# Slots made of two units of 256 edges in a graph kernel's gather stages, with attention's running totals added on TensorE

## The reference

```python
x = x + _L0_gnn_ref(_layernorm(x), src, dst, edge_weight, ...)   # segment_sum(val * n[dst], src), then a 256x256 matmul
x = x + _L0_ffn_ref(_layernorm(x)[None], ...)[0]                 # 16 experts, best 2
x = x + _L1_gnn_ref(_layernorm(x), ..., edge_attr_3, edge_index) # attention over edges, below
x = x + _L1_ffn_ref(_layernorm(x)[None], ...)[0]                 # 8 experts, best 1

# _L1_gnn_ref, H = 8 heads of D = 32
h_src = h[src]; h_dst = h[dst]
alpha = (h_src * a_src).sum(-1) + (h_dst * a_dst).sum(-1)
alpha = alpha + (relu(edge_attr @ edge_W.T + edge_b) * h_dst).sum(-1)
alpha = where(alpha >= 0, alpha, 0.2 * alpha)
ex = exp(alpha - segment_max(alpha, dst)[dst])
attn = ex / maximum(segment_sum(ex, dst)[dst], 1e-10)
out = segment_sum(h_src * attn, dst) + bias
```

## Time and profile before

| | us |
|---|---|
| median of 3 runs | 3073.1 |
| lowest, highest | 3066.4, 3090.2 |
| profiled execution | 3098.1 |
| its span | 3096.4 |
| PE busy (share of the span) | 2038.6 (66%) |
| DVE busy | 1689.1 (55%) |
| POOL busy | 1249.9 (40%) |
| ACT busy | 819.5 (26%) |
| `message_rows` | about 134 to 906 |
| `message_sums` | about 926 to 1151 |
| `attention` | about 1701 to 2625 |

### The profile page before, as it was taken

The page is one execution under the profiler, slowest core; times in us unless marked ns, Lnnn a source line. Parts: engine busy times, 40 slices in busy tenths (PEclk is TensorE's granted clock), DMA queues, the critical chain, the costliest instruction groups (busy, mean ns, idle before and its releaser), DMA issues. The chain is left out here.

```text
span 3096.4 us, 41327 instructions
## 1 busy us (share of the span) xinstructions
PE 2038.6 (66%) x12463; PEld 1551.3 (50%) x12552; DVE 1689.1 (55%) x3274; ACT 819.5 (26%) x2162; POOL 1249.9 (40%) x1222
## 2 busy tenths in 40 slices
PE   0256566555539996699623276667777766896995
PEld 0144444443427775599512155555555555235995
DVE  7644444444437778655576177666766767503222
ACT  5222222222210002233214033222333332432331
POOL 1166666666650000355303556456656651001221
PEclk9977676777769998799856588888988988898998
DMA  2144444444348862422321344344444442400113
GB/s 67 64 145 152 154 161 152 153 150 144 134 139 281 295 226 74 143 71 72 101 65 58 114 122 122 111 117 131 121 117 119 125 115 60 151 9 19 37 37 103
DMA packets 192121, 366.13 MB, mean 118 GB/s; under 512 B 47573, under 2 KB 102632, under 8 KB 191525
## 3 DMA queue, kind: packets, MB, share of 16 engines
q1 hardware_dynamic: 135472, 207.05, 20.9%
q0 software_dynamic: 56160, 156.43, 16.5%
q10 hardware_dynamic: 274, 0.00, 0.0%
HBM read 232.23 MB, written 131.07 MB: 117 GB/s over the span
## 5 line engine op out<-in xcount | busy, mean ns | idle before, releaser
L1945 POOL DMA_INDIRECT att_rows<-hdram,top_ix x488 | 502.2, 1029 | 375.6 <-DVE att_msg L2173 229.6
L767 POOL DMA_INDIRECT mtab<-msgs_rw,msgs_ix x488 | 486.6, 997 | 377.3 <-ACT msgs_rw L729 207.9
L656 PE MATMUL msgs_p_m<-nodes_n,msgs_hott 128*128 x976 | 364.1, 534 | 57.9 <-issue 42.5
L2017 PE MATMUL att_p_acc<-att_msg,att_hot 128*128 128x264 f32 x976 | 306.8, 468 | 100.6 <-ACT att_msg L2055 45.7
L589 DVE TENSOR_TENSOR msgs_rw<-msgs_p_m,msgs_sorted 128x1024 f32<-128x1024 f32 x122 | 149.3, 1224 | 376.2 <-remote 183.4
L656 PEld LDWEIGHTS msgs_p_m<-nodes_n,msgs_hott 128*128 128x128 f32 x976 | 248.9, 268 | 127.3 <-issue 82.1
L2017 PEld LDWEIGHTS att_p_acc<-att_msg,att_hot 128*128 128x128 f32 x976 | 211.1, 227 | 156.4 <-issue 88.6
L2047 ACT ACTIVATE att_enc<-att_p_z 128x1024 f32<-128x1024 f32 x122 | 124.8, 1023 | 586.8 <-remote 315.5
L2124 DVE TENSOR_TENSOR att_enc<-att_enc,att_p_h 128x1024 f32<-128x1024 f32 x122 | 148.8, 1219 | 224.2 <-remote 171.2
L837 PE MATMUL sums_part<-sums_rows,sums_hot 128*128 128x256 f32 x976 | 224.6, 390 | 34.0 <-DVE sums_hot L812 33.8
L1359 PE MATMUL exp_y<-exp_own,exp_ht 128*128 128x256 f32 x1032 | 239.0, 379 | 2.4 <-issue 2.4
(11 more groups left out here) (375 smaller groups left out, 3558.8 us busy)
## 6 DMA issues: line engine op xcount, KB each, us to landing
sums_rows<-mtab SPq DMA_DIRECT2D x122, 520.0 KB, 4.6
etab<-msgs_et SPq DMA_DIRECT2D x122, 288.0 KB
att_hz<-etab SPq DMA_DIRECT2D x122, 288.0 KB
first_w<-in_L_ffn_w SPq DMA_DIRECT2D x16, 512.0 KB
ffn0x_w<-in_L_ffn_w SPq DMA_DIRECT2D x16, 512.0 KB
ffn_w<-in_L_ffn_Wd SPq DMA_DIRECT2D x8, 1024.0 KB, 10.6
mtab<-msgs_rw,msgs_ix POOLq DMA_INDIRECT x488
att_rows<-hdram,top_ix POOLq DMA_INDIRECT x488
```

Source lines behind the costliest of these rows:

```text
L656: last = T.matmul(p_m[g % 2][:, q, :], hott[g % 2][:, q, :], node, start=True, stop=True)
L767: nc.gpsimd.indirect_dma_start(mtab, bass.IndirectOffsetOnAxis(ap=ix[:, g, q:q + 1], axis=0), rw[g % RS][:, q, :], None).then_inc(s_free[g ...
L1945: nc.gpsimd.indirect_dma_start(rows[:, g % RS, q, :], None, hdram, bass.IndirectOffsetOnAxis(ap=ix1[:, g, q:q + 1], axis=0)).then_inc(s_ro ...
L2017: last = T.matmul(p_acc[g % 2][:, 0:HW], hot[g % 2][:, q, :], msg[g % 2][:, q, :], start=(q == 0), stop=(q == G - 1))
```

## The change

A slot still has 512 edges and 4 columns, but it is two units of 256 edges (`U` = 2, `UE` = 256), and the two may belong to two different tiles. Tiles are padded to a multiple of 256 and not of 512, so that 220 units in `NS` = 110 slots do for the `dst` side. The `src` side keeps its 122 slots. What follows:

- `window_columns` and `window_rows` make the columns of the plan twice for `dst`, once for each unit of a slot. `gb` and the starts have one row of 110 for each unit.
- `message_rows`: SP loads a slot's records with two DMAs of half the size. PE reads two tile numbers for each slot, and the first two columns' matmuls take the one tile, the last two the other.
- `attention`, scores: likewise two tile numbers, `destinations` and `offsets` take two tiles. `maxima` compares 8 units and the one before (8 x 8 x 9 = 576 elements), and first makes the matrix of which units have different tiles (two small operations), which was made for all batches at the stage's start.
- `attention`, sums: `gathered` is gone from DVE. Each unit has its own PSUM buffer. PE adds the two columns of a unit and then the tile's old total, out of `acc`, by one more float32 matmul with the identity (`past`). For a batch's first unit the old total is the one that DVE multiplied by the fall (`fade`, once for a batch). ACT's `keep_total` copies each unit's PSUM buffer into `acc`, two copies for a slot, and at a batch's last unit one more into `total`.
- The order on ACT and PE is another: ACT does `weights` first, `keep_total` of the earlier slot's units before and behind `encodings`; PE does `past` of a slot's second unit between `encoders` and `destinations`, and `sums` ahead of `edge_tops`. `sums` waits until both units' copies of the slot before are done.

```diff
+U = 2
+UE = GE // U
+NS = ((E + NT * (UE - 1)) // UE + U - 1) // U
...
# window_columns
-    link(V.tensor_scalar(cmp[:], ends[:], ip, None, ALU.is_le))
+    for h in range(parts):
+        link(V.tensor_scalar(turn[:], cst["ip"][:], float(parts), float(h), ALU.mult, ALU.add))
+        link(V.tensor_scalar(cmp[:], ends[:], turn[:, 0:1], None, ALU.is_le))
...
# message_rows, load
-                sp.dma_start(sorted1[:, g, :], tab1[bass.ds(at, GE), :].rearrange("(p q) r -> p (q r)",
-                                                                                 p=P)).then_inc(s_tile[g % 8], 16)
+                for h in range(U):
+                    at = sp.value_load(starti[0:1, h * NS + g:h * NS + g + 1], min_val=0, max_val=E)
+                    sp.dma_start(sorted1[:, g, h * G // U * 8:(h + 1) * G // U * 8],
+                                 tab1[bass.ds(at, UE), :].rearrange("(p q) r -> p (q r)", p=P)).then_inc(s_tile[g % 8], 16)
...
# message_rows, products
+                for h in range(U):
+                    b = pe.value_load(gb[0:1, h * NS + g:h * NS + g + 1], min_val=0, max_val=NT - 1)
+                    nodes.append(n[:, bass.ds(b, 1), :].rearrange("p a c -> p (a c)"))
...
# attention, tensor
-                if g >= 2:
-                    pe.wait_ge(s_add, g - 1)
+                if g:
+                    pe.wait_ge(s_kept, U * g)
                 for q in range(G):
-                    last = T.matmul(p_acc[g % 2][:, 0:HW], hot[g % 2][:, q, :], msg[g % 2][:, q, :],
-                                    start=(q == 0), stop=(q == G - 1))
-                last.then_inc(s_acc, 1)
+                    T.matmul(p_acc[q * U // G][:, 0:HW], hot[g % 2][:, q, :], msg[g % 2][:, q, :],
+                             start=(q * U % G == 0), stop=False)
+                past(U * g)
+
+            def past(u):
+                if u % BU == 0:
+                    pe.wait_ge(s_faded, u // BU + 1)
+                    old = faded[:]
+                else:
+                    pe.wait_ge(s_kept, u)
+                    old = acc[:, bass.ds(held.pop(u), 1), :].rearrange("p a c -> p (a c)")
+                T.matmul(p_acc[u % U][:, 0:HW], cst["ident"][:], old, start=False, stop=True).then_inc(s_acc, 1)
...
# attention, tensor, the order of a step
+                if 0 <= s - LAG - 1 < NS:
+                    past(U * (s - LAG - 1) + 1)
+                if s + 1 < NS:
+                    nodes = destinations(s + 1)
...
# attention, scalar
-            def keep_total(g):
+            def keep_total(u):
...
-                act.wait_ge(s_add, g + 1)
-                if g:
-                    act.wait_ge(s_kept, g)
-                S.copy(acc[:, bass.ds(b, 1), :].rearrange("p a c -> p (a c)"), total[g % 2][:]).then_inc(s_kept, 1)
+                act.wait_ge(s_acc, u + 1)
+                if u % BU == BU - 1:
+                    S.copy(total[:], p_acc[h][:, 0:HW]).then_inc(s_total, 1)
+                S.copy(acc[:, bass.ds(b, 1), :].rearrange("p a c -> p (a c)"), p_acc[h][:, 0:HW]).then_inc(s_kept, 1)
...
# attention, vector
+            def fade(t):
+                dve.wait_ge(s_fall, t + 1)
+                if t:
+                    dve.wait_ge(s_total, t)
+                V.tensor_tensor(faded[:].rearrange("p (h d) -> p h d", d=D + 1), total[:].rearrange("p (h d) -> p h d", d=D + 1),
+                                bc(fall[t % 2][:], 2, D + 1), ALU.mult).then_inc(s_faded, 1)
```

262 lines of the change are left out of this document (129 added, 133 removed).

## The result

The changed kernel takes 3097.6 us in the median of 20 runs against 3075.2 us for the kernel before: a ratio of 1.0058, 95% interval 1.0044 to 1.0072. A second comparison (`after_again`) gave 1.0044 (1.0025 to 1.0062). Forecast were -0.6% and 3055 us; it is +0.6%, 43 us from the forecast. That is just above the forecast's own range (3015 to 3095 us), inside the one for 8 in 10, and on the other side of no change.

The account below looks back on a forecast made before the run. No engine was taken as the bound; chains of short waits set the slot periods. Message_rows -62, plan +4 and attention +40 gave -18 us on 3098.1, scaled by 0.992 to 3055 us (3015 to 3095; 8 in 10: 2944 to 3157).

Parts of the forecast that it names:

- Message_rows, -62 us: Message_rows: twelve slots fewer at 6.22 us give 75 us, less 13 us for the second tile number's read (-75 to -24).
- I take a quarter, 13 us: Message_rows: PE's second tile-number read, 0.46 us a slot, is exposed for a quarter, PE being busy 57% of the stage.
- the upper bound: Message_rows: all of the second read's 0.46 us exposed in each of 110 slots, 51 us.
- The smaller loads are hidden: Message_rows: SP's second DMA of a load costs nothing, since loads are issued twelve slots ahead.
- Attention's body, +40 us: Attention: twelve slots fewer give 83 us, but 107 periods grow by 1.15 us each, +123 us.
- the forecast's case: Attention: a slot costs 0.8 to 1.5 us more; chance 42%.
- the first rival: Attention: the additions hide in time already lost, a slot costs about 0.3 us more; -109 us, 2965 us; chance 30%.
- the identity matmuls with their wait: Attention: two identity matmuls a slot, +1.0 us of PE work, half taken as exposed: +0.5 us (0 to +1.0).
- the reads: Attention: two tile-number reads now behind the wait of `past`, 0.9 us, taken as +0.5 us a slot (0 to +0.9).
- The copy: Attention: ACT's copy of the first unit, 0.41 us, is covered by PE's other matmuls of 0.44 + 0.59 us.
- the slower rival: Attention: PE-ACT round trips become the period, a slot costs about 2.0 us more; +73 us, 3145 us; chance 28%.
- Late telling: Attention: PE's results are told late while POOL gathers, about 2.6 us of a slot's 6.92 us.

Follow-up runs that it names:

- after_again: The changed kernel, unchanged, run and profiled a second time: 1.0044 to the kernel before, 3085.5 us in its profile.
- b_number_early: Kernel before, with message_rows reading the tile number of slot g + 1 right behind the products of slot g: ratio 1.0006, 6.25 us for a slot.
- before_again: The kernel before, unchanged, profiled a second time: 3073.0 us, where its first profile had 3098.1 us.
- a_halves: Changed kernel, with the first unit's old total added between the halves of a slot's sums in attention: ratio 0.9985 to the kernel before.
- all_three: Changed kernel, tile numbers read early in message_rows and attention, first unit's old total added between the sums' halves: 0.9777 to the kernel before; repeated in another group, 0.9805.

## Why the prediction was wrong, step by step

By the pair of one group the sum came out at +12 us where it was -18. Two steps failed upwards, message_rows by 46 us and attention's end by 15, and attention's body, 23 us better than forecast, and the stretch ahead of attention, 6.5 us better, took back only a part.

- **Message_rows, -62 us, measured -16.** The failed step is "I take a quarter, 13 us". That slots keep their period was right but for the read: with it off the path the period is 6.29 us and the stage 64 us shorter than before (6.47 and 51 in the group of 3115 us). PE's busy share of the stage says nothing of whether its sequencer is next at that moment. The idle `issue` ahead of the products, 1.0 us for a slot before the change, hints that it often is, but gives no price: nearly half of it went away in `b_number_early` for nothing. In the changed kernel the cost was about the upper bound, 0.45 us for each slot, 49 us. The prediction's own criterion, more than half a microsecond, was met (0.53).
- **The smaller loads are hidden.** Hidden nearly in the steady slots (6.28 us for 6.20 to 6.22), but not at the start, where they are 4.4 us. Together 1.0023 (1.0001 to 1.0044), 0 to 14 us.
- **The plan, +4 us; attention's start unchanged.** +4.8 and +0.1. The first is right by luck: 3 us were for the new operations on DVE and 1 for the loads, but the loads alone give 4.4, and the operations nothing that shows (message_rows' first operation on DVE starts at 122.98 us before and 122.86 after).
- **Attention's body, +40 us, measured +17.** Growth is 0.91 us for a slot against `before_again`, 0.70 against the first profile and 0.59 at the least, where 1.15 was forecast. By 0.91 it lies in the forecast's case, by 0.70 in that of the first rival, which would have made the whole 2% faster; the sign was not lost here. Too high were the identity matmuls with their wait (0.5 given for the matmuls alone, 0.14 measured with the wait) and the reads (0.5; 0.09 for both put early). The maxima were 0.13 for 0.25. But terms priced one by one don't add: alone they give little more than half of the 0.65 that they make together, for which 1.25 was given. The copy was not covered as said: PE waits 67 us for copies in 720, 0.7 us for a slot, though taking one of the two waits away gave 0.13.
- **Attention's end: no term.** I multiplied the growth by 107 periods between activations, and gave nothing to the ten steps after the last one, where the matmuls with the identity and the round trips stand bare: +15 us at the full clock, +23 in the slower first profile. `a_halves` takes 8 of the 15 away.
- **The base.** I scaled the whole by 0.992 to come to the median. The profiled execution was slow in one stage: its body had 823.1 us, that of `before_again` 799.1 (message_rows 752.1 and 749.9). That is 24 of the 25 us between them, and 0.2 us of the growth's size. The other profiles with the old attention have 814, 819 and 837 us, so the 24 us lie within the spread of that stage over profiles and groups.
- **Signs.** 220 matmuls with the identity (0.61 us each with its two passes, for 0.5), DVE's busy time in the body down from 576 to 517 us, PE's up by 33, the granted clock from 0.87 to 0.90: as forecast. Periods of 6.3 and 8.1 us: both wrong, in opposite directions. PE's waits for ACT's copies ahead of `past` and `sums` showed up too, which the prediction gave as a sign of the slower rival; its period, near 9 us, did not.
- **Not forecast at all:** 6.5 us less between message_rows and attention; no run looked at it.
- **Late telling** was used as a fixed property of the kernel (2.6 us of each slot). It is absent in one of the groups, and there everything costs less: 5.52 us for a slot against 6.75 in message_rows.

## What to carry to other kernels

Where PE waits with nothing named ahead of a matmul, a further read of a register there can cost its full time (0.45 us for a slot here), half of it or nothing, and the idle time doesn't tell which. Move the read behind the previous matmuls and measure; the edit is a line. When a growth is multiplied by a number of periods, list what runs outside those periods: the drain of a pipeline has no cover, so a round trip that costs little in the steady state shows in full there. Profile the baseline more than once before pricing a change of 1%: one stage of it went from 799 to 837 us here.

## What the runs showed of the hardware

- While POOL issues gathers, other engines go on up to 33 us (DVE in the first profile of before) and 50 us (ACT in `before_again`, 1717.3 to 1767.0) after the recorded end of PE's matmuls in the result's runs and four groups, and at once in another; the kernel before takes 3075 to 3115 us in the former and 2730 in the latter.
- In the group of 2730 us `all_three` has message_rows at (699.9 - 142.6) / 109 = 5.11 us for a slot, four times POOL's 1.27 us for a scatter. With late telling and exposed reads gone, POOL's issue is the bound: of 540 us there it is busy for 413 and idle for 127, and 115 of these are the 0.30 us between two scatters, as its timeline shows:

```profile
400.17 0.97 POOL L791 DMA_INDIRECT mtab<-msgs_rw,msgs_ix  x1 [0.30 <-issue]
401.44 0.96 POOL L791 DMA_INDIRECT mtab<-msgs_rw,msgs_ix  x1 [0.30 <-issue]
```

- Loading a slot's records with two DMAs in place of one made the first records 4.4 us later, and the steady slots at most 0.1 us longer.
- One added wait of 1.5 us on PE in each slot went with a fall of the granted clock from 0.99 to 0.85; the slot went from 6.07 to 8.74 us.
